# A transformer layer on one core: layernorm transposes two chunks later, quantisation steps moved, FFN weights loaded in the last round

## Chip, cores and metric

One Trainium2 (trn2) chip, one core. The metric is the device time of one execution in microseconds; the number given is the median of several runs. The profile is of one further execution of the same program.

## The reference

x is (4, 1024, 256) in float32, 16 heads of 128, FFN width 1024.

```python
xn = _layernorm(x)
q, k, v = split(einsum("bsd,od->bso", xn, w_qkv))       # 3 x 16 heads x 128
q, k = _apply_rope(q), _apply_rope(k)
attn = softmax(q @ k^T / sqrt(128))
a = (attn @ v).reshape(B, S, 2048) @ w_out^T
q_up, s_up = quantize_to_mxfp4(up_kernel)               # blocks of 32 along K
h = gelu(xn @ (q_up * s_up) + up_bias)
q_dn, s_dn = quantize_to_mxfp4(down_kernel)
out = x + a + h @ (q_dn * s_dn) + down_bias
```

## The kernel before

**Staging.** The attention part runs over 4 sequences x 8 pairs of heads. Two pairs make a round (ROUNDS = 16), and a round has 16 chunks, k = 0 to 15; a pair has 8 chunks, k8 = k % 8 (four chunks of 256 queries for each of its two heads). In `steps` the first four chunks stand alone, then a loop over rounds, then the last chunks; every engine runs its own `step(i, k, first, last)` in this order, tied to the others by semaphores alone. After the attention comes the FFN, 8 groups of 512 tokens.

**One chunk on TensorE** (line 1057 on): the first score tile of the next chunk (`next_scores(0)`), whatever stands in slot 0, the second score tile, `output(c - 2)`, whatever stands in slot 1, and `values(k - 1)`. Values of a chunk are therefore computed one chunk after its scores' exponentials, and its output projection another chunk later. Output waits for o_lo, the low part of the values, which VectorE makes.

**What stands in the slots.** The table GROUPS, written out by hand, says for (k8, slot) which projection group of the next pair runs there: twelve per pair (qk0 0 to 3, v 0 to 3, qk1 0 to 3), with the number that orders them. LN_SLOT (2, 1) holds the transposes of the layernorm of two token tiles for the next sequence, once a round. MX_SLOT (10, 1) holds the transposes of the FFN weights of this round, which VectorE has quantised in eight parts, one in each of the chunks 2 to 9 (MX_PARTS).

**VectorE in a chunk** (step, line 825 on), in this order: turn the probabilities of chunk k (L690, four stream transposes), low part of o of chunk c-2 (L702), the maxima of the two score tiles (L680), reciprocal (L697), add the output to y (L713). Between the two maxima of k = 2 stand newton (L735 to L741, four tiny instructions in a chain) and normalise (L747, two). Behind add_out stand the mean (k = 0) and the quantise part of the chunk. `variance` is at k = 1. Each part of quantise is one to five instructions, each waiting for the one ahead (`link`).

**ScalarE in a chunk**: high part of the weights (`w_high`: qk0 and v at k8 = 0, qk1 at 4), high part of o (L588), copies of the slots' results (`take_group`; for qk groups three instructions, L572 to L574, which hand over to GpSimd), the squares of the layernorm (k = 1), two exponentials (L582).

**GpSimd**: low parts of the weights (`w_low`, L475: qk0 and v at k8 = 0), the layernorm's guess (L487, k = 1), and for each qk group a rotation of five instructions (L460 to L467). Scores of a head wait until all of its groups are rotated (`qk_ready`).

**SyncE** issues all DMAs, in order. Per chunk eight key moves (L355); then the loads of weights of the pair after next, the layernorm's and quantiser's loads and stores at k = 5 and 12. The FFN's biases, x for the FFN (`load_x(0)`) and the two quantised weights come behind the last chunk (lines 414 to 423).

**Prologue**: ten projection groups of the first pair in FIRST_BANKS, ahead of the first scores. FIRST_HELD says which group must have been copied out before its bank is used again.

Of the kernel before, what the change touches and what calls it, by code (L numbers as in the profile page):

```python
# [8 lines left out]
F32 = mybir.dt.float32  # L9
# [7 lines left out]
BATCH, SEQ, DIM = 4, 1024, 256  # L17
HEADS, HEAD = 16, 128
FF = 1024
P = 128  # L20
# [9 lines left out]
PAIRS = BATCH * HEADS // 2  # L30
PAIRS_PER_SEQ = HEADS // 2
# [3 lines left out]
PAIR_GROUPS = 12  # L35
# [4 lines left out]
MX_COLS = 2 * DIM * FF // P  # L40
ROUNDS = PAIRS // 2
# [5 lines left out]
def layer(nc, d):  # L47
# [7 lines left out]
    with ExitStack() as ctx:  # L55
# [6 lines left out]
        def pb(name, shape):  # L62
# [36 lines left out]
        ln_x = sb("ln_x", [P, LN_STEP, DIM])  # L99
# [38 lines left out]
        o_ps = pb("o_ps", [P, 512])  # L138
        w_ps = pb("w_ps", [P, 512])
        FIRST_BANKS = [w_ps[:, :], o_ps[:, :], s_ps[1][:, 0:512], s_ps[1][:, 512:1024], slot_ps[:, 0], slot_ps[:, 1],  # L140
                       w_ps[:, :], o_ps[:, :], slot_ps[:, 0], s_ps[1][:, 0:512]]
        FIRST_HELD = {6: 0, 7: 1, 8: 4, 9: 2}

        const_loaded = sem("const_loaded")
        ident_loaded = sem("ident_loaded")
# [69 lines left out]

        GROUPS = {(3, 0): (0, "qk0", 0), (3, 1): (1, "qk0", 1), (4, 0): (2, "qk0", 2), (4, 1): (3, "v", 0),
                  (5, 0): (4, "qk0", 3), (5, 1): (5, "v", 1), (6, 0): (6, "v", 2), (6, 1): (7, "v", 3),
                  (7, 0): (8, "qk1", 0), (7, 1): (9, "qk1", 1), (0, 0): (10, "qk1", 2), (1, 0): (11, "qk1", 3)}  # L220
        FIRST_GROUPS = sorted(GROUPS.values())[:10]

        LN_SLOT, MX_SLOT = (2, 1), (10, 1)
        MX_PARTS = (2, 3, 4, 5, 6, 7, 8, 9)

        def group_at(k, slot, last):

# [55 lines left out]
        def _(sp):  # L283
            def load_part(p, pw, part, first=False):
                if not first:
                    sp.wait_ge(w_lo_ready[part], p)
                    sp.wait_ge(w_hi_ready[part], p)
                sp.dma_start(w_raw[:, :, PARTS[part]], d["w_qkv"][pw][:, :, PARTS[part]]).then_inc(w_loaded[part], 16)
# [25 lines left out]
            def load_mx(i):  # L314

                sp.dma_start(mx_raw[:, :], d["mx_rows"][:, bass.ds(i * MX_STEP, MX_STEP)]).then_inc(mx_loaded, 16)
# [42 lines left out]
            def batch(b, first, last):  # L359

                for n in range(SEQ_CHUNKS):
                    p, j, k8 = b * PAIRS_PER_SEQ + n // 8, n // 8, n % 8
                    r, k = b * SEQ_ROUNDS + n // 16, n % 16
                    move_chunk(b * SEQ_CHUNKS + n, n, first)
                    if not first:
                        if 1 <= n <= QUARTERS:
                            sp.wait_ge(y_stored, (b - 1) * (QUARTERS * 16) + 16 * n)
                            load_y(b, n - 1)
                        if n < QUARTERS:
                            store_y(b - 1, n)  # L370
                    if k8 == 1:
                        if j == PAIRS_PER_SEQ - 1 and not last:
                            sp.wait_ge(ln_stored, (b + 1) * (SEQ_ROUNDS * 32))
                            sp.wait_ge(proj_ready, (b + 1) * (PAIRS_PER_SEQ * PAIR_GROUPS))
                            load_x(b + 1)
                        if not (last and j >= PAIRS_PER_SEQ - 2):
                            load_part(p + 2, (j + 2) % PAIRS_PER_SEQ, "qk0")
                            load_part(p + 2, (j + 2) % PAIRS_PER_SEQ, "v")
                    if k8 == 5 and not (last and j >= PAIRS_PER_SEQ - 2):
                        load_part(p + 2, (j + 2) % PAIRS_PER_SEQ, "qk1")  # L380
                    if k8 == 4 and not (last and j == PAIRS_PER_SEQ - 1):
                        load_wo(p + 1, (j + 1) % PAIRS_PER_SEQ, 1)
                    if k8 == 7 and not (last and j >= PAIRS_PER_SEQ - 2):
                        load_wo(p + 2, (j + 2) % PAIRS_PER_SEQ, 0)
                    last_round = last and n // 16 == SEQ_ROUNDS - 1
                    if k == 5:
                        store_ln(r)
                        if not last_round:
                            load_ln(r + 1)
                    if k == 12:  # L390
                        store_mx(r)
                        if not last_round:
                            load_mx(r + 1)

            batch(0, True, False)
            for b in range(1, BATCH - 1):
# [14 lines left out]
                sp.wait_ge(rows_ready, (g + 1) * 2)  # L411
                sp.dma_start(d["out"][:, bass.ds(g * GT, GT), :], y_out[:, n]).then_inc(out_stored[n], 16)

            sp.dma_start(up_bias[:, :], d["up_bias"]).then_inc(bias_loaded, 16)
            sp.dma_start(down_bias[:, :], d["down_bias"].to_broadcast([P, DIM])).then_inc(bias_loaded, 16)
            sp.wait_ge(proj_ready, PAIRS * PAIR_GROUPS)
            sp.wait_ge(ln_stored, ROUNDS * 32)
            load_x(0)
            sp.wait_ge(mx_stored, ROUNDS * 16)
            for n in range(2):  # L420
                cols = slice(n * MX_COLS // 2, (n + 1) * MX_COLS // 2)
                dst = (up_w[:, :], down_w)[n]
                sp.dma_start(dst.bitcast(F32), d["mx"][:, cols]).then_inc(mx_w_loaded[n], 16)
            sp.wait_ge(scores_ready, TOK * HEADS // P)
            load_seq(1)
            load_seq(2)
# [43 lines left out]
        def _(pool):  # L470
# [31 lines left out]
            def step(i, k, first, last):  # L502
                if k >= 16:
                    return
                k8 = k % 8
                more = not (last and k >= 8)
                p = i * 2 + k // 8
                if k8 == 0 and more:
                    w_low(p + 1, "qk0")
                    w_low(p + 1, "v")  # L510
                if k8 == 3:
                    wo_low(p, 1)
                if k8 == 4 and more:
                    w_low(p + 1, "qk1")
                if k8 == 6 and more:
                    wo_low(p + 1, 0)
                if k == 1:
                    guess(i + 2, LN_COLS)
                for slot in (0, 1):
                    g = group_at(k, slot, last)  # L520
                    if g and g[1] != "v":
                        p = i * 2 + g[3]
                        rotate(pool, nc.gpsimd, p, g[1], g[2], "pool", p * 8 + qk_number(g[1], g[2]) - 3).then_inc(qk_ready, 1)
# [13 lines left out]
        def _(act):  # L537
            def w_high(p, part, first=False):

                cols = PARTS[part]  # L540
                act.wait_ge(w_loaded[part], (p + 1) * 16)
                if not first:
                    act.wait_ge(proj_ready, p * 12 - (0 if part == "qk1" else 4))
                nc.scalar.activation(w_hi[:, :, cols], w_raw[:, :, cols], ACT.Copy).then_inc(w_hi_ready[part], 1)

            def wo_high(p, h, first=False):
# [68 lines left out]
            def step(i, k, first, last):  # L615
# [4 lines left out]
                tail = last and k >= 16  # L620
                if k % 8 == 0 and more and not tail:
                    w_high(p + 1, "qk0")
                    w_high(p + 1, "v")
                if k % 8 == 3:
                    wo_high(p, 1, first)
# [15 lines left out]
                    act.wait_ge(mx_turned_ready, i + 1)  # L641
                    nc.scalar.activation(mx_turned[:, :], slot_ps[:, 1, 0:MX_STEP], ACT.Copy).then_inc(mx_copied, 1)
                if not tail:
                    if k == 1:
                        squares(i + 2, ln_x, LN_COLS)
                    if not (last and k == 15):
                        exponentials(t + 2, 2 * k + 2, first and k == 0)
                    g = group_at(k, 0, last)
                    if g:
                        take_group(i * 2 + g[3], *g[:3], g[3] % 2, slot_ps[:, 0])  # L650
                    if not (last and k == 15):
                        exponentials(t + 3, 2 * k + 3, first and k == 0)
                if k == 14:
                    act.wait_ge(ln_stored, (i + 1) * 32)
                    act.wait_ge(mx_stored, (i + 1) * 16)

# [19 lines left out]
        def _(dve):  # L676
# [152 lines left out]
            def step(i, k, first, last):  # L829
# [12 lines left out]
                                            ln_hi[:, :, :].bitcast(F32), ALU.subtract).then_inc(ln_lo_ready, 1)  # L842
                if not tail and not (last and k == 15):
                    row_max(t + 2, 2 * k + 2)
                if k == 1:
                    variance(LN_COLS, i * LN_STEP + BT)
                if k == 2:
                    newton(i + 2, LN_COLS)
                    normalise(i + 2, ln_x, ln_xn, LN_COLS)
                if not tail and not (last and k == 15):  # L850
                    row_max(t + 3, 2 * k + 3)
                if has_out:
                    invert(c - 2, 2 * k - 4)
                    add_out(c - 2, (k - 2) % 16, (i // 4) if k >= 2 else ((i - 1) // 4))
                if k == 0:
                    dve.wait_ge(ln_loaded, (i + 1) * 16)
                    mean(i + 2, ln_x, LN_COLS)
                if k in MX_PARTS:
                    quantise(i, MX_PARTS.index(k))

            steps(dve, step)

# [40 lines left out]
        def _(pe):  # L903
# [140 lines left out]
            pe.wait_ge(first_keys_pool, 1)  # L1044
            scores(0, 0, False)
            pe.wait_ge(rope_in, 6)
            pe.wait_ge(v_ready, 1)
            scores(1, 0, False)

            def step(i, k, first, last):  # L1050
# [11 lines left out]
                def slot(n):  # L1062
# [18 lines left out]
                        return  # L1081
                    place, part, num, ahead = g
                    if first and k == 0:
                        pe.wait_ge(rope_in, 6)
                        pe.wait_ge(v_ready, 4)
                    else:
                        bank_free(i, k, n, first, last)
                    if num == 0:
# [91 lines left out]
```

## Time and profile before

| | |
|---|---|
| median of 3 runs | 2652.19 us (2650.29 to 2653.58) |
| profiled execution, its own time | 2650.27 us |
| its span | 2648.5 us |
| PE busy | 2489.9 us, 94% |
| DVE busy | 2047.9 us, 77% |
| POOL busy | 1836.1 us, 69% |
| ACT busy | 1356.4 us, 51% |
| mean granted clock of TensorE | 0.979 |

The span goes from the first to the last instruction; the execution's own time has 1.8 us around it. PE is TensorE's matmuls, PEld its weight loads, DVE VectorE, ACT ScalarE, POOL GpSimd, SP SyncE and SPq its DMA queue. L702 is line 702 of the kernel. Many matmuls stand under the helper's line, L907, and are told apart by their tile: s_ps scores, w_ps output, o_ps values, slot_ps what runs in the slots. Busy times of PE are modelled at their ends and overlap a little with the next group's start, so PE's times are best read from start to start.

### The profile page before, as it was taken

The page shows a single profiled execution, that of the slowest core. Times are in us where ns is not written, and L with a number is a line of the kernel's source. Part 1 is how long each engine was busy: PE and PEld are TensorE (multiplying, and loading weights), DVE is VectorE, ACT ScalarE, POOL GpSimd, SP SyncE. Part 2 cuts the span into 40 slices and gives each one's busy share as a digit, 9 for nine tenths or more (in the row PEclk, how much of TensorE's full clock was granted, in tenths as well). Part 3 has the DMA queues.
Part 4 walks back from the last instruction along what each step waited for, and adds up shares of the span by engine and source line. Part 5 has one row for each costly group of instructions (what it writes and reads, how often), then busy time and mean ns, then how long its engine had stood idle before and what let it go on. Part 6 is the DMA issues. An engine that isn't in the chain of part 4 may idle for free. (4 is left out here: it accounts for less than half of the span.)

```text
span 2648.5 us, 42033 instructions
## 1 busy us (share of the span) xinstructions
PE 2489.9 (94%) x12656; PEld 2157.4 (81%) x12656; DVE 2047.9 (77%) x3209; ACT 1356.4 (51%) x2518; POOL 1836.1 (69%) x1480
## 2 busy tenths in 40 slices
PE   5999999999999999999999999999999999999799
PEld 4887878888787888878788887878888787887688
DVE  6868778786877878787787878778687877868676
ACT  5555545555554555555455555545555454554333
POOL 6677767867776776787677678767767876776221
PEclk9999999999999999999999999999999999999999
DMA  3555545545654554546555454546555454544642
GB/s 105 135 132 132 136 105 153 129 119 162 161 138 105 150 128 121 132 127 169 136 152 128 121 134 125 138 110 171 137 150 136 123 138 112 144 121 111 189 172 64
DMA packets 233732, 354.30 MB, mean 134 GB/s; under 512 B 37840, under 2 KB 95440, under 8 KB 233424
## 3 DMA queue, kind: packets, MB, share of 16 engines
q1 hardware_dynamic: 233680, 353.72, 51.5%
q8 instruction: 18, 0.29, 0.0%
q14 instruction: 34, 0.28, 0.0%
HBM read 66.26 MB, written 18.87 MB: 32 GB/s over the span
## 5 line engine op out<-in xcount | busy, mean ns | idle before, releaser
L907 PE MATMUL o_ps<-keys_first,v_rows 128*128 128x256 f32 x4096 | 950.9, 386 | 0.0
L582 ACT ACTIVATE probs<-s_ps,neg_max 128x1024 f32<-128x1024 f32 x512 | 571.2, 1116 | 664.2 <-DVE neg_max L680 658.2
L680 DVE TENSOR_REDUCE neg_max<-s_ps 128x1 f32<-128x1024 f32 x512 | 621.5, 1219 | 341.9 <-PE s_ps L907 341.5
L907 PEld LDWEIGHTS o_ps<-keys_first,v_rows 128*128 128x128 f32 x4096 | 782.9, 195 | 105.9
L907 PE MATMUL s_ps<-seq_parts 128*128 128x512 f32 x3072 | 828.6, 407 | 36.9 <-POOL seq_parts L467 25.4
L907 PEld LDWEIGHTS s_ps<-seq_parts 128*128 128x128 f32 x3072 | 575.0, 188 | 160.7 <-POOL seq_parts L467 31.4
L460 POOL TENSOR_TENSOR rope_a<-rope_a,cos 128x512 f32<-128x512 f32 x253 | 329.4, 1302 | 541.6 <-ACT rope_b L574 541.6
L690 DVE STREAM_TRANSPOSE turned_blocks<-probs 128x512 f32<-128x512 f32 x1024 | 637.3, 679 | 26.5 <-DVE mx_inv L778 9.9
L907 PE MATMUL slot_ps<-seq_parts,w_parts 128*128 128x512 f32 x1512 | 388.7, 392 | 1.5 <-ACT probs L574 1.5
L588 ACT ACTIVATE o_hi<-o_ps 128x256 fp32r<-128x256 f32 x256 | 98.5, 385 | 525.2 <-PE o_ps L907 525.2
L465 POOL TENSOR_TENSOR rope_a<-rope_a,rope_b 128x512 f32<-128x512 f32 x253 | 330.7, 1307 | 19.8
L463 POOL TENSOR_TENSOR seq_parts<-rope_a,rope_b 128x512 fp32r<-128x512 f32 x253 | 327.8, 1296 | 19.8
L467 POOL TENSOR_TENSOR seq_parts<-rope_a,seq_parts 128x512 fp32r<-128x512 f32 x253 | 327.0, 1292 | 19.8
L461 POOL TENSOR_TENSOR rope_b<-rope_b,sin 128x512 f32<-128x512 f32 x253 | 330.6, 1307 | 0.0
L907 PEld LDWEIGHTS slot_ps<-seq_parts,w_parts 128*128 128x128 f32 x1512 | 280.6, 189 | 59.9 <-issue 1.7
L713 DVE SCALAR_TENSOR_TENSOR y<-w_ps,inv_sum,y 128x256 f32<-128x256 f32 x512 | 224.4, 480 | 45.3 <-PE w_ps L907 17.0
L702 DVE TENSOR_TENSOR o_lo<-o_ps,o_hi 128x256 fp32r<-128x256 f32 x256 | 102.9, 402 | 130.8 <-ACT o_hi L588 130.8
L907 PE MATMUL slot_ps<-w_parts,seq_parts 128*128 128x256 f32 x1500 | 200.3, 283 | 0.0
L907 PEld LDWEIGHTS slot_ps<-w_parts,seq_parts 128*128 128x128 f32 x1500 | 191.0, 191 | 2.6
L573 ACT ACTIVATE rope_b<-slot_ps 64x512 f32<-64x512 f32 x251 | 149.3, 595 | 3.0
L574 ACT ACTIVATE rope_b<-slot_ps 64x512 f32<-64x512 f32 x251 | 148.1, 590 | 2.9
L572 ACT ACTIVATE rope_a<-slot_ps 128x512 f32<-128x512 f32 x251 | 148.0, 590 | 1.2 <-DVE seq_parts L467 1.2
(109 smaller groups left out, 2159.2 us busy)
## 6 DMA issues: line engine op xcount, KB each, us to landing
keys_first<-turned_blocks SPq DMA_DIRECT2D x2048, 128.0 KB, 2.7
w_raw<-in_w_qkv SPq DMA_DIRECT2D x96, 256.0 KB, 3.2
seq_parts<-xnt_parts SPq DMA_DIRECT2D x14, 1024.0 KB, 7.9
wo_raw<-in_w_out SPq DMA_DIRECT2D x64, 128.0 KB, 2.5
y<-in_x SPq DMA_DIRECT2D x16, 256.0 KB, 3.2
ln_x<-in_x SPq DMA_DIRECT2D x16, 256.0 KB, 3.8
xnt_parts<-ln_hi SPq DMA_DIRECT2D x16, 256.0 KB, 3.3
xnt_parts<-ln_lo SPq DMA_DIRECT2D x16, 256.0 KB, 3.6
```

The source lines that it names most:

```text
L460: engine.tensor_tensor(a, a, cos[:, cols], ALU.mult).then_inc(own, 1)
L461: engine.tensor_tensor(b, b, sin[:, cols], ALU.mult).then_inc(own, 1)
L463: engine.tensor_tensor(hi, a, b, ALU.add).then_inc(own, 1)
L465: engine.tensor_tensor(a, a, b, ALU.add).then_inc(own, 1)
L467: return engine.tensor_tensor(lo, a, hi.bitcast(F32), ALU.subtract)
L573: nc.scalar.activation(b[0:h], bank[h:P], ACT.Copy, scale=scale)
L574: nc.scalar.activation(b[h:P], bank[0:h], ACT.Copy, scale=scale).then_inc(rope_in, 1)
L582: nc.scalar.activation(probs[:, k2 % 4, :], s_ps[k2 % 2][:, :], ACT.Exp, bias=neg_max[:, col:col + 1], accum_out=row_sum[:, col:col + 1]). ...
L680: nc.vector.tensor_reduce(neg_max[:, k2 % 16:k2 % 16 + 1], s_ps[k2 % 2][:, :], AXX, ALU.max, negate=True).then_inc(max_ready, 1)
L690: last = nc.vector.transpose(turned_blocks[:, k % 2, 2 * half:2 * half + 2, :, n, :].rearrange("p b j q -> p j b q"), keys)
L713: last = nc.vector.scalar_tensor_tensor(rows, w_ps[:, n * DIM:(n + 1) * DIM], inv_sum[:, col:col + 1], rows, ALU.mult, ALU.add)
L907: ins = nc.tensor.matmul(out, w, m, start=(n == 0), stop=(n == len(terms) - 1))
```

## The change

- GROUPS: v 0 goes from (4, 1) to (5, 1), v 1 from (5, 1) to (6, 0), v 2 from (6, 0) to (6, 1), and v 3 from (6, 1) into the next pair, to (0, 1). The prologue has nine groups.
- LN_SLOT goes from chunk 2 to chunk 4. The mean goes from k = 0 to 1, the squares, variance and guess from 1 to 2. Newton and normalise go from k = 2, between the maxima, to k = 3, behind add_out. The store and next load of the layernorm go from k = 5 to 6.
- MX_PARTS: the eight parts stand in the chunks 3 to 7: 0 and 1 at 3, then 2, 3, 4 and 5, 6 and 7.
- The v part of the weights is loaded at k8 = 3 (was 1) and split at k8 = 2 (was 0).
- The loads of the FFN's biases, of x and of the FFN weights are issued at k = 10, 11 and 13 of the last round, and not behind it. ScalarE's wait for the stores goes from k = 14 to 15.

```diff
-        GROUPS = {(3, 0): (0, "qk0", 0), (3, 1): (1, "qk0", 1), (4, 0): (2, "qk0", 2), (4, 1): (3, "v", 0),
-                  (5, 0): (4, "qk0", 3), (5, 1): (5, "v", 1), (6, 0): (6, "v", 2), (6, 1): (7, "v", 3),
-                  (7, 0): (8, "qk1", 0), (7, 1): (9, "qk1", 1), (0, 0): (10, "qk1", 2), (1, 0): (11, "qk1", 3)}
-        FIRST_GROUPS = sorted(GROUPS.values())[:10]
-
-        LN_SLOT, MX_SLOT = (2, 1), (10, 1)
-        MX_PARTS = (2, 3, 4, 5, 6, 7, 8, 9)
+        GROUPS = {(3, 0): (0, "qk0", 0), (3, 1): (1, "qk0", 1), (4, 0): (2, "qk0", 2), (5, 0): (3, "qk0", 3),
+                  (5, 1): (4, "v", 0), (6, 0): (5, "v", 1), (6, 1): (6, "v", 2), (7, 0): (7, "qk1", 0),
+                  (7, 1): (8, "qk1", 1), (0, 0): (9, "qk1", 2), (0, 1): (10, "v", 3), (1, 0): (11, "qk1", 3)}
+        FIRST_GROUPS = sorted(GROUPS.values())[:9]
+
+        USED = {"qk0": 4, "v": 11, "qk1": 12}
+
+        LN_SLOT, MX_SLOT = (4, 1), (10, 1)
+        MX_PARTS = {3: (0, 1), 4: (2,), 5: (3,), 6: (4, 5), 7: (6, 7)}
...
                             load_part(p + 2, (j + 2) % PAIRS_PER_SEQ, "qk0")
-                            load_part(p + 2, (j + 2) % PAIRS_PER_SEQ, "v")
+                    if k8 == 3 and not (last and j >= PAIRS_PER_SEQ - 2):
+                        load_part(p + 2, (j + 2) % PAIRS_PER_SEQ, "v")
...
-                    if k == 5:
+                    if k == 6:
                         store_ln(r)
...
+                    if last_round and k == 10:
+                        sp.dma_start(up_bias[:, :], d["up_bias"]).then_inc(bias_loaded, 16)
+                        sp.dma_start(down_bias[:, :], d["down_bias"].to_broadcast([P, DIM])).then_inc(bias_loaded, 16)
+                    if last_round and k == 11:
+                        sp.wait_ge(proj_ready, PAIRS * PAIR_GROUPS)
+                        sp.wait_ge(ln_stored, ROUNDS * 32)
+                        load_x(0)
+                    if last_round and k == 13:
+                        sp.wait_ge(mx_stored, ROUNDS * 16)
+                        for m in range(2):
+                            cols = slice(m * MX_COLS // 2, (m + 1) * MX_COLS // 2)
+                            dst = (up_w[:, :], down_w)[m]
+                            sp.dma_start(dst.bitcast(F32), d["mx"][:, cols]).then_inc(mx_w_loaded[m], 16)
...
                 if k8 == 0 and more:
                     w_low(p + 1, "qk0")
+                if k8 == 2 and more:
                     w_low(p + 1, "v")
...
-                if k == 1:
+                if k == 2:
                     guess(i + 2, LN_COLS)
...
-                if k == 1:
+                if k == 2:
                     variance(LN_COLS, i * LN_STEP + BT)
-                if k == 2:
-                    newton(i + 2, LN_COLS)
-                    normalise(i + 2, ln_x, ln_xn, LN_COLS)
                 if not tail and not (last and k == 15):
                     row_max(t + 3, 2 * k + 3)
                 if has_out:
                     invert(c - 2, 2 * k - 4)
                     add_out(c - 2, (k - 2) % 16, (i // 4) if k >= 2 else ((i - 1) // 4))
-                if k == 0:
+                if k == 1:
                     dve.wait_ge(ln_loaded, (i + 1) * 16)
                     mean(i + 2, ln_x, LN_COLS)
-                if k in MX_PARTS:
-                    quantise(i, MX_PARTS.index(k))
+                if k == 3:
+                    newton(i + 2, LN_COLS)
+                    normalise(i + 2, ln_x, ln_xn, LN_COLS)
+                for part in MX_PARTS.get(k, ()):
+                    quantise(i, part)
```

ScalarE's `w_high` of v goes to k8 = 2 and its squares to k = 2, as the same kind of edit; in the prologue TensorE's waits for the copies of v follow the new order.

## Rows read from the trace of the kernel before

**Rows 1.** The page, part 1: busy us, share of the span, instructions.
```profile
PE 2489.9 (94%) x12656; PEld 2157.4 (81%) x12656; DVE 2047.9 (77%) x3209; ACT 1356.4 (51%) x2518; POOL 1836.1 (69%) x1480
```

**Rows 2.** Waits: engine, line, waited for: us in total, times, longest.
```profile
PE slot_ps L1068 <- DVE ln_xn L747: 86.5, 16, 5.6
...
PE s_ps L907 <- POOL seq_parts L467: 25.4, 15, 1.7
...
PE s_ps L1008 <- DMA up_w<-mx_blocks: 12.6, 1, 12.6
```

**Rows 3.** Timeline of PE: transposes, scores of chunk 3, transposes a round later.
```profile
687.32 1.12 PE L1068 MATMUL slot_ps<-ident,ln_xn 128*128 128x128 f32 x4 [5.59 <-DVE ln_xn L747]
...
692.43 1.75 PE L907 MATMUL s_ps<-seq_parts 128*128 128x512 f32 x6
...
841.45 1.12 PE L1068 MATMUL slot_ps<-ident,ln_xn 128*128 128x128 f32 x4 [5.60 <-DVE ln_xn L747]
```

**Rows 4.** Windows: length, busy time by engine, granted clock, DMA share, GB/s.
```profile
687.30:692.43 5.13, 5.11 (x20) 4.47 (x21) 4.70 (x10) 1.51 (x3) 0.72 (x1) 0.73 0.26 93
```

**Rows 5.** Timeline of PE, chunk 4: scores, output, v group, values.
```profile
702.11 1.72 PE L907 MATMUL s_ps<-seq_parts 128*128 128x512 f32 x6
...
706.39 0.28 PE L907 MATMUL w_ps<-wo_hi,o_hi 128*128 128x256 f32 x1
...
707.11 1.60 PE L907 MATMUL slot_ps<-w_parts,seq_parts 128*128 128x256 f32 x12
708.55 3.62 PE L907 MATMUL o_ps<-keys_first,v_rows 128*128 128x256 f32 x16
```

**Rows 6.** Timeline of PE: output of chunk 10, scores of chunk 11.
```profile
760.59 0.39 PE L907 MATMUL w_ps<-wo_hi,o_hi 128*128 128x256 f32 x1
...
766.94 1.66 PE L907 MATMUL s_ps<-seq_parts 128*128 128x512 f32 x6 [1.70 <-POOL seq_parts L467]
```

**Rows 7.** Timeline of POOL: low parts of qk0 and v at k8 = 0.
```profile
751.04 2.54 POOL L475 TENSOR_TENSOR w_parts<-w_raw,w_parts 128x512 fp32r<-128x512 f32 x2
```

**Rows 8.** Timeline of DVE: newton to the next maxima, part 0, part 1, two turns.
```profile
680.82 1.07 DVE L735 TENSOR_TENSOR ln_step<-ln_guess 128x2 f32<-128x2 f32 x1
681.92 1.19 DVE L737 TENSOR_TENSOR ln_step<-ln_step,ln_var 128x2 f32<-128x2 f32 x1
...
687.18 1.21 DVE L680 TENSOR_REDUCE neg_max<-s_ps 128x1 f32<-128x1024 f32 x1
...
689.51 0.28 DVE L768 TENSOR_SCALAR mx_abs<-mx_raw 128x256 uint32<-128x256 uint32 x1
...
690.39 2.49 DVE L690 STREAM_TRANSPOSE turned_blocks<-probs 128x512 f32<-128x512 f32 x4
...
699.13 0.74 DVE L772 TENSOR_SCALAR mx_amax<-mx_amax 128x8 f32<-128x8 f32 x1
...
703.11 2.49 DVE L690 STREAM_TRANSPOSE turned_blocks<-probs 128x512 f32<-128x512 f32 x4 [0.66 <-DVE mx_inv L778]
...
757.75 2.48 DVE L690 STREAM_TRANSPOSE turned_blocks<-probs 128x512 f32<-128x512 f32 x4
```

**Rows 9.** Single lines: least/median/most ns, first and last start, forms.
```profile
L737 DVE TENSOR_TENSOR ln_step<-ln_step,ln_var x18: 161/1186/1191, 9.6 to 2384.2; 128x2 f32<-128x2 f32 x16, 128x4 f32<-128x4 f32 x2
...
L764 DVE SCALAR_TENSOR_TENSOR mx_q<-mx_abs,mx_q x96: 411/907/1520, 100.0 to 2450.9; 128x256 f32<-128x256 f32 x96
```

**Rows 10.** Timeline of POOL: beside newton, and the first rotation of chunk 3.
```profile
681.83 1.27 POOL L461 TENSOR_TENSOR rope_b<-rope_b,sin 128x512 f32<-128x512 f32 x1
...
698.56 1.28 POOL L460 TENSOR_TENSOR rope_a<-rope_a,cos 128x512 f32<-128x512 f32 x1 [7.82 <-ACT rope_b L574]
```

**Rows 11.** Key moves of the last three chunks (SyncE), and all key moves' landing.
```profile
2482.57 18.94 SPq L355 DMA_DIRECT2D keys_first<-turned_blocks  x24
...
DMA to landing us min/median/max: 2.5/2.7/7.1
```

**Rows 12.** Timeline of PE, first round, scores at k = 1.
```profile
54.10 2.93 PE L907 MATMUL s_ps<-seq_parts 128*128 128x512 f32 x6 [9.65 <-ACT probs L582]
```

More of the change, by code:

```diff
@@ L140, in layer @@
         FIRST_BANKS = [w_ps[:, :], o_ps[:, :], s_ps[1][:, 0:512], s_ps[1][:, 512:1024], slot_ps[:, 0], slot_ps[:, 1],
-                       w_ps[:, :], o_ps[:, :], slot_ps[:, 0], s_ps[1][:, 0:512]]
-        FIRST_HELD = {6: 0, 7: 1, 8: 4, 9: 2}
+                       w_ps[:, :], o_ps[:, :], s_ps[1][:, 0:512]]
+        FIRST_HELD = {6: 0, 7: 1, 8: 2}
         const_loaded = sem("const_loaded")
@@ L412, in store_rows @@
                 sp.dma_start(d["out"][:, bass.ds(g * GT, GT), :], y_out[:, n]).then_inc(out_stored[n], 16)
[L414 to L423, printed above, removed]
             sp.wait_ge(scores_ready, TOK * HEADS // P)
@@ L542, in w_high @@
                 if not first:
-                    act.wait_ge(proj_ready, p * 12 - (0 if part == "qk1" else 4))
+                    act.wait_ge(proj_ready, (p - 1) * 12 + USED[part])
                 nc.scalar.activation(w_hi[:, :, cols], w_raw[:, :, cols], ACT.Copy).then_inc(w_hi_ready[part], 1)
@@ L622, in step @@
                     w_high(p + 1, "qk0")
+                if k % 8 == 2 and more:
                     w_high(p + 1, "v")
@@ L652, in step @@
                         exponentials(t + 3, 2 * k + 3, first and k == 0)
-                if k == 14:
+                if k == 15:
                     act.wait_ge(ln_stored, (i + 1) * 32)
@@ L844, in step @@
                     row_max(t + 2, 2 * k + 2)
-                if k == 1:
+                if k == 2:
                     variance(LN_COLS, i * LN_STEP + BT)
-                if k == 2:
-                    newton(i + 2, LN_COLS)
-                    normalise(i + 2, ln_x, ln_xn, LN_COLS)
                 if not tail and not (last and k == 15):
@@ L1046, in _ @@
             pe.wait_ge(rope_in, 6)
-            pe.wait_ge(v_ready, 1)
             scores(1, 0, False)
@@ L1083, in slot @@
                     if first and k == 0:
-                        pe.wait_ge(rope_in, 6)
-                        pe.wait_ge(v_ready, 4)
+                        pe.wait_ge(v_ready, n + 1)
                     else:
```

## The prediction, made before the changed kernel was run

> **What bounds the kernel now.** The first view to read is the busy time by engine: PE 2489.9 us of a span of 2648.5 [rows 1]. So the time is PE's work and PE's waits, and another engine counts only where it makes PE wait. The second view is the waits [rows 2]: three cost PE something. Once a round, sixteen times, the layernorm transposes wait for VectorE's ln_xn, 86.5 us together; 5.59 each [rows 3], so that 2.7 is left for the first round. Fifteen times scores wait 1.7 us for the rotation on GpSimd, 25.4 together. Once the FFN waits 12.6 us for the load of up_w. VectorE (77%) is no bound on average, but it works in order, and a burst of work on it makes it late.
>
> The third view is PE's timeline in a steady round. Call Sk the start of the first scores of chunk k. The transposes of k=2 start at 687.32, those of the next round at 841.45: a round is 154.1 us [rows 3]. The fourth view is the windows: behind the wait the granted clock is 0.73 for 5.13 us, that is partly 1.2 GHz instead of 2.4 after PE had stood idle; 5.13 x 0.27 = 1.4 us lost besides [rows 4].
>
> **Part by part.** PE does the same twelve groups per pair and the same transposes; work 0. What moves is one v group, 708.55 - 707.11 = 1.44 us [rows 5], from chunks 4 and 12 to 0 and 8.
>
> *The wait for GpSimd.* At k=11 scores waited 1.70 us for the last instruction of the last qk1 rotation [rows 6]. The change takes the low part of v, half of 2.54 = 1.27 us [rows 7], from ahead of that rotation, and PE comes 1.44 later by the v group that now stands at k=8. 1.70 - 1.27 - 1.44 = -1.0: the wait goes, and it does not appear at k=3, where the other wait hid it until now and where the guess too has left its place. Gain 25 us. With rotations slowed by VectorE some of it could stay: bounds 18 and 25.
>
> *The wait for ln_xn* at k=2 goes: 86.5 us, and the low clock behind it, 15 x 1.4 = 21.
>
> *What is late next.* VectorE's step 3 now ends with newton, normalise and quantise parts 0 and 1, one behind the other. Their prices, each up to the start of what came behind: newton and normalise 687.18 - 680.82 = 6.36; part 0 690.39 - 689.51 = 0.88; part 1 703.11 - 699.13 = 3.98, 0.66 of it idle for its last link [rows 8]. Sum 11.2. They are so dear because GpSimd works beside them: L737 takes 161 ns at least but 1186 in the median [rows 9], and it ended at 683.11 as GpSimd's instruction of 681.83 did, at 683.10 [rows 8, 10]. GpSimd works in step 3 as well: it starts the rotation of (3, 0) at S3 + 6.13 (698.56 - 692.43), and that of (3, 1) follows, ten instructions of 1.3 us [rows 3, 10]. VectorE's added work starts at S3 + 6.70 (699.13 - 692.43). So I take the dear prices. Part 0 stood beside an idle GpSimd until now; if its first instruction has to wait too, the sum is 11.8. I take 11.4.
>
> Who waits for that: VectorE begins step 4 at S3 + 18.1. Ahead of the low part of o it turns the probabilities; from the start of the turn at 757.75 to PE's output matmul at 760.59 it was 2.84 [rows 6, 8]. So output starts at S3 + 20.9, which is S4 + 11.3, as chunk 3 lasts 9.68 (702.11 - 692.43). PE gets there at S4 + 4.28 (706.39 - 702.11) [rows 3, 5]. It stalls 7.0 us in each round, and will show this as "w_ps waits for o_lo". 16 x 7.0 = 112 us, and the low clock behind it, 16 x 1.4 = 22. Queued behind the output on PE are the transposes (which find ln_xn long ready), the values and the next scores; ScalarE and VectorE wait for these in turn, so that the whole chunk ends 7 us later and VectorE has caught up. With what went, a round is again about 154 us.
>
> The Trainium skill, "SBUF — State Buffer", section "Who interferes with whom", has a rule that speaks against this change: GpSimd and some VectorE instructions (two SBUF inputs, or a tensor_scalar in a fast form) share a port pair under an exclusive lock, the loser is blocked for a whole instruction, and tensor_reduce never is. By that rule nine added instructions of step 3 wait for one of GpSimd's each: an estimate of 9 x 1.3 and 0.9 for the others, 12.6, and a stall of 8.2.
>
> *Later chunks.* Step 4 keeps part 2; VectorE begins step 5 about when PE begins chunk 5, and its turn is covered until S5 + 4.28. Steps 5, 6 and 7 have two, four and four instructions of quantise. L764, the commonest, takes 0.91 us in the median [rows 9]: 3.6 for four. From 6.7 into the chunk, and with 2.84 for the turn, output could start 13.2 after Sk, where PE comes at 9.7 + 4.28 = 14.0. No second stall, by 0.8 us.
>
> *Queues of ScalarE and SyncE.* ScalarE, 51% busy [rows 1], has w_high of v and the squares one or two chunks later; both fall in time in which it waits for the maxima: 0. Its wait for the stores comes at k=15, three chunks behind them: 0. SyncE issues the v load behind the key moves of chunk 3; 24 key moves took 18.9 us, at most 6.3 a chunk [rows 11], of chunks that last 9.7 where the v load stands, and the load is used a pair later: 0. Uncovered it would be some 3 us, once a pair.
>
> *Start.* A v projection leaves the prologue. PE then waits 9.65 us all the same for ScalarE's exponentials behind VectorE's rotation [rows 12], so 0; bounds -3 and +2, since ScalarE's copies change their order.
>
> *End.* x and the FFN weights are loaded at k=11 and 13, not behind the key moves of chunk 15. The 12.6 us of [rows 2] go, and about 1.3 of low clock. But 4 MB now run beside the key moves of chunks 12 to 14, and values wait for those; a key move landed in 2.7 us in the median, 7.1 at most [rows 11]. Bounds of the loss: 0, and twice 4.4. I take 2. Gain 12.
>
> **Sum**, against the profiled execution's own 2650.3 us (the span and 1.8 around it; the median of the runs is 1.9 above it): -86.5 - 21 - 25 + 112 + 22 - 12 = -10.5, so 2639.8, and 2641.7 on the median's scale. As starts measured from start to start lose slightly more than the idle times I took off, I round this down to 2640. One microsecond of the stall is worth 16.
>
> **Rivals.**
> (a) *The added work hides.* If GpSimd did not hold VectorE up, the small instructions would cost 0.2 us and the wide ones 0.41 [rows 9], about 3.5 in all: output could start at S3 + 6.7 + 3.5 + 0.7 + 2.8 = S4 + 4.0, ahead of PE. The 134 us are not added: 2506. For it: the chunks from 3 on are the long ones. Against it: the same instructions beside the same rotation in [rows 8, 10]. Cases half-way, some instructions slipping in between two of GpSimd's, give 2560 to 2600. Chance 0.14 together.
> (b) *Slower: a second stall.* Its place is steps 6 and 7 with four quantise instructions each. At the 1.52 that L764 takes at most [rows 9] each step has 6.1 instead of 3.6: output is ready 15.6 after Sk, 1.6 late, once or twice a round, less what the first lateness covers. From 0.9 us a round on, first stall or second, all the gain and 0.2% more is gone. With 1.5: 2640 + 24 = 2664. Against it: in chunk 6 GpSimd has ended its rotations before VectorE comes to the quantise parts. Chance 0.13.
> (c) *No change.* The loads of the end hold the key moves up by twice 4.4 us, and 0.3 us of the rotation wait stays: 2640 + 7 + 5 = 2652. Chance 0.12.
> My forecast has 0.61. That the transposes were not moved off the wait can be left out: by the sum ln_xn is ready 8 us before them.
>
> **Numbers.** A measurement of this kernel can tell 0.2%, 5 us, from no change. The stall's bounds are 5.8 (small instructions slipping in) and 8.2: -19 and +19 us; clock 0.8 to 2.0 a stall, -10 and +10; the end -2 and +7. Together 2615 to 2664. The range goes down for part of the half-way cases and holds (c) and half of (b): 2598 to 2664. Faster: 0.44 of my forecast's 0.61, (a) 0.14, a little of (c), in all 0.62. Same 0.22, slower 0.16.
>
> **What would show it.** Right: PE waits neither for ln_xn nor for GpSimd's seq_parts; sixteen waits of w_ps for o_lo of about 7 us, all at k=4; L735 starts 6.7 us after S3, L737 still takes 1.2, the turn of step 4 starts 18 after S3; up_w is there before PE. Wrong: a round of 145 to 147 us (a: I priced step 3 wrongly); waits for o_lo more than once a round (b); values waiting for key moves in the last chunks (c); or another waiter than output at k=4, the second scores for instance, which would mean that I named the wrong path.

## The result, and the profile after

The changed kernel takes 2656.39 us (median of 20 runs, 2649.71 to 2660.54), the kernel before 2651.16 (20 runs, 2649.97 to 2653.58). The ratio is 1.0016, with a 95% interval of 1.0010 to 1.0023: slower, by 0.16%. The forecast was 2640, so nearly half a percent faster. The profiled execution took 2657.86 us, with a span of 2656.1.

The page's busy times of the changed kernel, to set against [rows 1]:

```profile
PE 2497.0 (94%) x12656; PEld 2166.2 (82%) x12656; DVE 2038.3 (77%) x3209; ACT 1357.1 (51%) x2518; POOL 1826.7 (69%) x1480
```

PE does the same 12656 matmuls, with the same share of the span. What changed is the list of its waits (engine, line, waited for: us in total, times, longest), to set against [rows 2]:

```profile
PE w_ps L915 <- DVE o_lo L710: 123.6, 33, 7.4
PE s_ps L1042 <- DVE probs L755: 14.3, 2, 12.2
PE s_ps L915 <- ACT probs L589: 7.1, 1, 7.1
PE o_ps L915 <- DMA keys_first<-turned_blocks: 4.1, 2, 3.3
PE s_ps L915 <- DVE seq_parts L473: 3.2, 1, 3.2
```

All three waits of [rows 2] that cost PE something are gone: 86.5 + 25.4 + 12.6 = 124.5 us. In their place PE waits 123.6 us for o_lo, which was 1.0 before: 16 waits of 6.9 to 7.4 at the output of chunk 4 and 16 of some 0.34 at chunk 8, one of each a round. The timeline of PE in a steady round shows where: chunk 4 (S4 = 702.73) and chunk 8.

```profile
702.73 1.72 PE L915 MATMUL s_ps<-seq_parts 128*128 128x512 f32 x6
...
714.54 0.58 PE L915 MATMUL w_ps<-wo_hi,o_hi 128*128 128x256 f32 x1 [7.37 <-DVE o_lo L710]
...
721.84 1.74 PE L915 MATMUL s_ps<-seq_parts 128*128 128x512 f32 x6
...
755.87 0.39 PE L915 MATMUL w_ps<-wo_hi,o_hi 128*128 128x256 f32 x1 [0.34 <-DVE o_lo L710]
```

Scores in chunks 3 (693.06) and 4 start without a wait, so GpSimd's last rotation is in time. The output of chunk 4 waits 7.37 us. VectorE's timeline of the same stretch says why. Read each start against the one ahead of it: from newton's first instruction at 699.75, right behind add_out, to the turn at 711.61 stands one chain of thirteen instructions, and only behind the turn comes o_lo (L710).

```profile
699.75 0.61 DVE L743 TENSOR_TENSOR ln_step<-ln_guess 128x2 f32<-128x2 f32 x1
700.39 1.20 DVE L745 TENSOR_TENSOR ln_step<-ln_step,ln_var 128x2 f32<-128x2 f32 x1
701.62 0.17 DVE L747 TENSOR_SCALAR ln_step<-ln_step 128x2 f32<-128x2 f32 x1
...
702.97 2.83 DVE L755 TENSOR_SCALAR ln_xn<-ln_x,ln_mean,ln_rstd 128x256 f32<-128x256 f32 x2
705.73 1.38 DVE L776 TENSOR_SCALAR mx_abs<-mx_raw 128x256 uint32<-128x256 uint32 x1
...
711.61 2.49 DVE L698 STREAM_TRANSPOSE turned_blocks<-probs 128x512 f32<-128x512 f32 x4 [0.66 <-DVE mx_inv L786]
714.03 0.39 DVE L710 TENSOR_TENSOR o_lo<-o_ps,o_hi 128x256 fp32r<-128x256 f32 x1
```

Step 3's chain starts 6.69 us after S3 and lasts 11.86. GpSimd's timeline beside it: the rotation of (3, 0) runs from 699.07 on, instruction by instruction, and L745 ends at 701.59 as GpSimd's instruction of 700.30 does at 701.57. Not every instruction is held up: L747 starts at 701.62, between the end of one of GpSimd's at 701.57 and the start of the next at 701.65, and takes 0.17 us.

```profile
699.07 1.28 POOL L466 TENSOR_TENSOR rope_a<-rope_a,cos 128x512 f32<-128x512 f32 x1 [4.37 <-ACT rope_b L581]
700.30 1.27 POOL L467 TENSOR_TENSOR rope_b<-rope_b,sin 128x512 f32<-128x512 f32 x1
701.65 1.26 POOL L469 TENSOR_TENSOR seq_parts<-rope_a,rope_b 128x512 fp32r<-128x512 f32 x1
```

At chunk 8 the small wait has the same form: parts 6 and 7 stand beside the rotation of (7, 0), whose first instruction starts at 747.41, and the turn comes late.

```profile
748.23 0.61 DVE L803 TENSOR_SCALAR mx_raw<-mx_raw 128x256 uint32<-128x256 uint32 x1
748.76 1.49 DVE L772 SCALAR_TENSOR_TENSOR mx_q<-mx_abs,mx_q 128x256 f32<-128x256 f32 x1
...
753.02 2.48 DVE L698 STREAM_TRANSPOSE turned_blocks<-probs 128x512 f32<-128x512 f32 x4
```

**The account by stages**, each between two landmarks of PE that both kernels have (before minus after, spans of 2648.5 and 2656.1):

| stage | before | after | difference |
|---|---|---|---|
| start, to the scores of k=2 of the first round | 63.71 | 65.95 | +2.2 |
| rounds, to the mx transposes of the last | 2400.63 | 2414.95 | +14.3 |
| from there to the first down matmul | 61.56 | 52.58 | -9.0 |
| FFN, to the end | 122.6 | 122.6 | 0 |

### The profile page after: what moved, and what is told of

It is laid out like the page before. It is cut to its first block and busy times, and to the rows that moved or that the text cites. A ratio compares the mean times of both kernels' runs of the same rounds, so it can differ in the third digit from the quotient of the medians.

```text
span 2656.1 us, 41956 instructions
## 1 busy us (share of the span) xinstructions
PE 2497.0 (94%) x12656; PEld 2166.2 (82%) x12656; DVE 2038.3 (77%) x3209; ACT 1357.1 (51%) x2518; POOL 1826.7 (69%) x1480
## 5 line engine op out<-in xcount | busy, mean ns | idle before, releaser
L915 PE MATMUL w_ps<-wo_hi,o_hi 128*128 128x256 f32 x512 | 152.4, 298 | 123.7 <-DVE o_lo L710 123.6
L915 PEld LDWEIGHTS w_ps<-wo_hi,o_hi 128*128 128x128 f32 x512 | 100.9, 197 | 147.0 <-issue 116.5
L710 DVE TENSOR_TENSOR o_lo<-o_ps,o_hi 128x256 fp32r<-128x256 f32 x256 | 104.2, 407 | 128.2 <-ACT o_hi L595 125.7
L580 ACT ACTIVATE rope_b<-slot_ps 64x512 f32<-64x512 f32 x250 | 148.7, 595 | 3.0
```

The costliest lines, as they stand in the source:

```text
L580: nc.scalar.activation(b[0:h], bank[h:P], ACT.Copy, scale=scale)
L710: nc.vector.tensor_tensor(as_queries(o_lo[:, slot, :]), as_quadrants(o_ps[:, 0:CHUNK]), as_queries(o_hi[:, slot, :].bitcast(F32)), ALU.sub ...
L915: ins = nc.tensor.matmul(out, w, m, start=(n == 0), stop=(n == len(terms) - 1))
```

## The experiments

Every run stands beside runs of the kernel before on the same chip, whose medians were 2650.8 to 2651.9 us.

**Is GpSimd what makes the chain long?** The rotations of slots (3, 0) and (3, 1) work on 8 columns instead of 512, so that most of these query and key parts are left out; VectorE's program is the same.

```diff
-    rotate(pool, nc.gpsimd, p, g[1], g[2], "pool", p * 8 + qk_number(g[1], g[2]) - 3).then_inc(qk_ready, 1)
+    rotate(pool, nc.gpsimd, p, g[1], g[2], "pool", p * 8 + qk_number(g[1], g[2]) - 3,
+           8 if k == 3 else HALF).then_inc(qk_ready, 1)
```

> The changed kernel, but the GpSimd rotations of the groups in slots (3, 0) and (3, 1) of each round work on 8 columns instead of 512 (most of these query and key parts are left out). VectorE's work in step 3 is untouched. Theory (GpSimd holds VectorE up): the chain behind add_out shrinks from 11.9 to about 4 us, output of chunk 4 no longer waits, 2495 to 2520 us. Rival (VectorE's chain is that long by itself): the chain stays 11 to 12 us, the stall stays at 7, about 2650 us.

Measured: 2500.1 us, ratio 0.9434 (0.9418 to 0.9449). VectorE's timeline of step 3:

```profile
658.09 0.15 DVE L744 TENSOR_TENSOR ln_step<-ln_guess 128x2 f32<-128x2 f32 x1
...
658.88 0.73 DVE L756 TENSOR_SCALAR ln_xn<-ln_x,ln_mean,ln_rstd 128x256 f32<-128x256 f32 x2
659.53 0.29 DVE L777 TENSOR_SCALAR mx_abs<-mx_raw 128x256 uint32<-128x256 uint32 x1
...
661.15 0.17 DVE L787 TENSOR_SCALAR mx_inv<-mx_inv 128x8 f32<-128x8 f32 x1
661.99 2.49 DVE L699 STREAM_TRANSPOSE turned_blocks<-probs 128x512 f32<-128x512 f32 x4 [0.67 <-DVE mx_inv L787]
```

The same instructions take 3.90 us instead of 11.86, GpSimd's beside them 0.2 us each, and the wait of chunk 4 is gone. This settles the question: two thirds of the chain was time in which GpSimd held VectorE up. The Trainium skill's rule of the exclusive port pair ("SBUF — State Buffer", "Who interferes with whom") agrees with this pair of runs, also in that the reduction among them kept its 0.42 us. By the rule the prediction had estimated 12.6 us for the chain, 0.7 above the 11.86 of the trace, in which L747 and L782 passed at 0.17 us each.

**Which work belongs where?** Newton and normalise put between the two maxima of chunk 3, where GpSimd is idle:

```diff
                 if k == 2:
                     variance(LN_COLS, i * LN_STEP + BT)
+                if k == 3:
+                    newton(i + 2, LN_COLS)
+                    normalise(i + 2, ln_x, ln_xn, LN_COLS)
                 if not tail and not (last and k == 15):
                     row_max(t + 3, 2 * k + 3)
...
-                if k == 3:
-                    newton(i + 2, LN_COLS)
-                    normalise(i + 2, ln_x, ln_xn, LN_COLS)
```

> The changed kernel with newton and normalise of step 3 put between the two maxima of chunk 3, where GpSimd is idle (its low parts end 1.6 us after S3, its rotation starts 6.0 after it) and VectorE waits 1.5 us for scores anyway. Theory (VectorE's chain in step 3 is dear because GpSimd's rotation holds it up): L745 falls from 1.2 us to about 0.2 and L755 from 1.4 to 0.4; only parts 0 and 1 (5.9 us) are left behind add_out, the stall of w_ps at k=4 shrinks from 7.4 to about 2 us and most of the low clock behind it goes: about 2540 us. Rival (the chain is dear by itself, whatever GpSimd does): L745 and L755 stay, the second maximum comes 4.5 us late, the stall stays at about 6: about 2640 us.

Measured: 2517.7 us, ratio 0.9498 (0.9482 to 0.9514), 22 better than expected. VectorE's timeline in chunk 3:

```profile
658.27 0.15 DVE L743 TENSOR_TENSOR ln_step<-ln_guess 128x2 f32<-128x2 f32 x1
658.45 0.16 DVE L745 TENSOR_TENSOR ln_step<-ln_step,ln_var 128x2 f32<-128x2 f32 x1
...
659.05 0.74 DVE L755 TENSOR_SCALAR ln_xn<-ln_x,ln_mean,ln_rstd 128x256 f32<-128x256 f32 x2
659.87 1.23 DVE L688 TENSOR_REDUCE neg_max<-s_ps 128x1 f32<-128x1024 f32 x1
```

Newton and normalise take 1.6 us, in place of 5.98, and fill a gap in which VectorE had waited for scores. The stall at k=4 is 0.8 us, 1.2 less than the 2 expected, which is 19 us in sixteen rounds. Half of that is parts 0 and 1, which I took at their full 5.9 and which came to 5.3.

**The other half: quantise moved away from chunk 3**, newton left behind add_out:

```diff
-        MX_PARTS = {3: (0, 1), 4: (2,), 5: (3,), 6: (4, 5), 7: (6, 7)}
+        MX_PARTS = {4: (0,), 5: (1,), 6: (2, 3, 4), 7: (5,), 8: (6,), 9: (7,)}
```

> The changed kernel with the quantise parts spread over chunks 4 to 9 (part 0 at 4, 1 at 5, 2 to 4 at 6, 5 at 7, 6 at 8, 7 at 9), none in chunk 3. Theory (the lateness is the length of the chain in step 3): newton and normalise alone take 6.0 us, the stall at k=4 becomes 6.7 + 6.0 + 2.9 - 13.95 = 1.6 us, the 0.34 at k=8 goes: about 2530 us. Rival (the layernorm sets the stall and the quantiser only fills idle time): stall unchanged near 7, about 2650 us.

Measured: 2528.2 us, ratio 0.9534 (0.9518 to 0.9550). Its stall at k=4 is 1.47 us (expected 1.6), and it has 0.3 us at k=10:

```profile
676.21 0.38 PE L915 MATMUL w_ps<-wo_hi,o_hi 128*128 128x256 f32 x1 [1.47 <-DVE o_lo L710]
676.42 0.28 PE L915 MATMUL w_ps<-wo_lo,o_hi 128*128 128x256 f32 x1
...
677.46 3.62 PE L915 MATMUL o_ps<-keys_first,v_rows 128*128 128x256 f32 x16
680.72 1.75 PE L915 MATMUL s_ps<-seq_parts 128*128 128x512 f32 x6
```

Behind this short wait the next matmuls soon stand 0.12 us apart and the values take 3.26 us, full clock, and so in all sixteen rounds. Either half alone removes most of the loss, as neither half of the chain is long enough by itself to pass the cover of 4.4 us by much. That is why the halves' gains (139 and 128 us) do not add up.

**Both edits together.**

> Both edits: newton and normalise between the maxima of chunk 3, quantise spread over chunks 4 to 9. Theory: no step of VectorE is late, no wait of PE in the steady rounds, a round of about 145 us instead of 155.3: 2656 - 16 x 10.2 = about 2493 us. Rival (another limit stands close behind, for example GpSimd's rotation ahead of the scores of k=3 or the key moves): a round of 148 us or more, 2540 us or more, with a wait of another name.

Measured: 2501.5 us, ratio 0.9432 (0.9416 to 0.9448). No wait at k=4, a round of 145.4 us. The expectation of 2493 left out 0.32 us at k=10 in every round, the place that e2 had shown too, and the start, whose scores of k=2 come at 64.66 us in this profile and at 62.81 in e4_narrow's.

**Parts 6 and 7 both in chunk 8**, which is a long chunk since it holds a v group:

```diff
-        MX_PARTS = {4: (0,), 5: (1,), 6: (2, 3, 4), 7: (5,), 8: (6,), 9: (7,)}
+        MX_PARTS = {4: (0,), 5: (1,), 6: (2, 3, 4), 7: (5,), 8: (6, 7)}
```

> As e3_both, but quantise parts 6 and 7 both in chunk 8, which is a long one now, and none in 9. Theory: the last wait of a steady round, 0.32 us at the output of chunk 10 behind part 7 of chunk 9, goes with nothing in its place: 145.0 us a round, 16 x 0.4 = 7 us less than e3_both, about 2495 us. Rival (parts 6 and 7 together are too long for step 8): a wait at the output of chunk 9 instead, 2501 us or more.

Measured: 2493.7 us, ratio 0.9407 (0.9393 to 0.9422). The busy time of PE over fifteen rounds (window; length, busy time by engine, clock, DMA share, GB/s):

```profile
83.90:2259.50 2175.60, 2173.59 (x11133) 1892.64 (x11132) 1701.05 (x2836) 1217.69 (x2281) 1702.25 (x1366) 1.00 0.56 143
```

PE idles 2 us in 2176, nearly all of it in three waits for a load of seq_parts, 1.9 us together. That is what is left to gain by waits in the rounds: next to nothing. A round has 145.0 us, and so the 154.1 of [rows 3] held 9 to 10 us of stalls and low clock, of which the change had merely renamed the most part.

**Does an idle PE pay twice?** In the changed kernel 24 matmuls that nobody reads run ahead of chunk 4's output, in PE's idle time:

```diff
+                if k == 4:
+                    bank_free(i, k, 1, first, last)
+                    for m in range(24):
+                        nc.tensor.matmul(slot_ps[:, 1], qk_hi[:, 1, 0, 0:P], qk_hi[:, 1, 1, 0:HALF], start=True, stop=True)
                 if not (first and k < 2):
                     output(c - 2, (k - 2) % 16, i * 2 + (k - 2) // 8, first and k == 2)
```

> The changed kernel with 24 more matmuls of 512 columns (a scores product once more, written to the free slot bank and never read) ahead of the output of chunk 4, in time in which PE stands idle for o_lo. Nothing else is changed. Theory (the idle time costs a second time, through the granted clock behind it, about 2.3 us a round): output, transposes and values of chunk 4 take 4.4 us instead of 6.2 to 7.3, a round is 153 us, about 2620 us, although PE does 82 us more work. Rival (low clock is not due to the idle time, or the added work delays the output): 2656 us or more.

Measured: 2626.4 us, ratio 0.9908 (0.9893 to 0.9923). PE does more and is 30 us faster than in the changed kernel. Its longest wait for o_lo is 2.1 us now, and the mean granted clock of the core is 0.995 where it was 0.970.

```profile
PE w_ps L915 <- DVE o_lo L710: 37.9, 33, 2.1
```

The low clock behind the wait is thus worth about 30 us a run, 1.9 a round. It is not gone everywhere: in four of the sixteen rounds output, transposes and values still take 6.1 us behind a wait of 2.0, in the others 4.5. For the changed kernel the windows behind the wait of chunk 4 show it, here in a steady round and in the first:

```profile
714.54:721.84 7.30, 7.30 (x26) 6.40 (x27) 6.20 (x11) 4.08 (x7) 3.21 (x3) 0.60 0.72 189
94.10:101.01 6.91, 6.91 (x26) 6.14 (x27) 6.19 (x11) 4.08 (x7) 2.82 (x3) 0.64 0.70 171
```

Long and short stretches take turns: the one a round after the first of these, from the output at 870.38 to the next scores at 876.58, takes 6.20 us at a granted clock of 0.71. At full clock the same output, transposes and values take 4.4 us, so that the low clock costs 1.5 to 2.9 us a round.

**The loads of the end by themselves**, on the kernel before:

```diff
+                    if last_round and k == 11:
...
+                        load_x(0)
+                    if last_round and k == 13:
...
-            load_x(0)
-            sp.wait_ge(mx_stored, ROUNDS * 16)
```

> The kernel before with only the loads of the end moved into the last round (biases at k=10, x at 11, FFN weights at 13). Theory: from the mx transposes of the last round to the first down matmul the changed kernel took 52.6 us instead of 61.6, so this part alone is worth 9 us: about 2642 us, the wait for up_w gone, 3 to 4 us of values waiting for key moves in its place. Rival (the gain came with the rest of the change): 2651 us, or no waits for key moves at all and 2639.

Measured: 2642.3 us, ratio 0.9968 (0.9955 to 0.9981). The change's end part alone is worth 8.5 us, and values wait 3.0 us for key moves, here at the two chunks whose moves run beside the loads. The eight moves issued behind the two loads of x landed in 7.4 us in the median, where 2.7 was the median of all in the kernel before:

```profile
2489.97 5.41 PE L911 MATMUL o_ps<-keys_first,v_rows 128*128 128x256 f32 x16 [2.41 <-DMA keys_first<-turned_blocks]
...
2504.87 3.72 PE L911 MATMUL o_ps<-keys_first,v_rows 128*128 128x256 f32 x16 [0.58 <-DMA keys_first<-turned_blocks]
```

**The start.** Twelve idle matmuls ahead of the first scores of the changed kernel, while PE waits for the rotation:

```diff
+            for m in range(12):
+                nc.tensor.matmul(s_ps[0][:, 0:HALF], x_hi[:, 0, 0:P], x_hi[:, 0, 0:HALF], start=True, stop=True)
             pe.wait_ge(first_qk_dve, 2)
```

> The changed kernel with 12 idle matmuls of 512 columns ahead of the first scores, into their own bank, in time in which PE waits 3.2 us for the rotation. Theory (the start lost 2.2 us since PE, with one group less, stood idle and had the low clock from 34 us on): the twelve matmuls of the second scores take 3.0 us instead of 5.3, the scores of k=2 start about 2 us earlier, 2654 us. Rival (the new order of ScalarE's copies made the start late): the start stays, 2656 us.

Measured: 2654.4 us (11 runs), ratio 1.0015 (1.0006 to 1.0024). The interval covers the changed kernel's, so the median does not tell the two apart. The traces do differ. The changed kernel, and then this one:

```profile
38.87 5.49 PE L915 MATMUL s_ps<-seq_parts 128*128 128x512 f32 x12 [0.80 <-ACT rope_b L581]
...
65.95 3.10 PE L915 MATMUL s_ps<-seq_parts 128*128 128x512 f32 x12
```

```profile
38.19 3.00 PE L915 MATMUL s_ps<-seq_parts 128*128 128x512 f32 x12 [2.07 <-ACT rope_b L581]
...
62.66 3.08 PE L915 MATMUL s_ps<-seq_parts 128*128 128x512 f32 x12
```

The scores of the second tile ran at low clock in the changed kernel's profiled execution and at full clock here, and k=2 starts 3.3 us earlier. But the other traces spread as widely without this edit. With the changed prologue as it is, k=2 starts at 62.3 to 62.8 us in five of them (e1_between, e4_narrow, e6_busy_wait, e8_spread, e8_again) and at 65.05 and 64.66 in e2_quant_away and e3_both; with the prologue of before it starts at 63.71 and, in e5_end_loads_only, at 65.41. Low clock in the twelve matmuls is not enough for a late start: in e8_spread they took 4.25 us, and k=2 came at 62.30. In the three late traces of the changed prologue the first six score matmuls, from 35 us on, had also run at low clock, 2.8 to 2.9 us instead of 1.67. So the start differs from one execution to the next by as much as the 2.2 us of the account; that the change costs anything there is not shown.

**Both ends mended**: e8_spread with the start of e7 and with down_w loaded at k=14.

> e8_spread with both ends mended: the twelve idle matmuls of e7_start_busy ahead of the first scores, and the second FFN weight (down_w) loaded at k=14 of the last round instead of behind up_w at k=13. Theory: e8's profile already had the full clock at its start, so the first edit is worth 0 to 3 us in the median; the second takes 1 to 2 us from the 4.4 us in which values wait for key moves, since each load then stands beside the moves of one chunk: 2489 to 2493 us. Rival (the key moves wait for the bytes ahead of them, whatever their order, or down_w comes late for the first down matmul): 2494 us or more, with the same 4.4 us or a new wait of s_ps for w_parts.

Measured: 2491.9 us, ratio 0.9401 (0.9386 to 0.9417). Beside it:

> e8_spread once more, beside e9_ends on the same chip: 2493 us in the median, to be set against e9_ends.

Measured: 2495.4 us, ratio 0.9409 (0.9393 to 0.9425). The waits of values for key moves, first e9_ends, then e8_again:

```profile
PE o_ps L915 <- DMA keys_first<-turned_blocks: 2.7, 4, 1.2
```

```profile
PE o_ps L915 <- DMA keys_first<-turned_blocks: 7.4, 2, 5.0
```

The wait is shorter and the medians differ by 3.5 us, but the intervals overlap, and e8_spread, the same kernel as e8_again, waited 4.4 us for key moves and had a median of 2493.7. So a gain by the later load is possible, not shown. The idle matmuls brought nothing that the traces show: k=2 starts at 63.38 in e9_ends and at 62.81 in e8_again. The expectation also took e8_spread's start for one at full clock, which its twelve matmuls of 4.25 us were only in part. e9_ends has the lowest median found, 6% below both kernels, and it leaves out nothing of the computation.

## Why the prediction was wrong

*The mechanism was right, point by point.* The waits for ln_xn, for GpSimd's rotation and for up_w went. VectorE's step 3 became late, its added work started at S3 + 6.69 (forecast 6.70), and PE stalled at the output of chunk 4, once a round, for o_lo. Rival (a), that the added work hides, was refused by the trace, and e4_narrow shows its condition: with GpSimd's instructions cut to 0.2 us beside the chain it does hide, at 2500 us (2506 was worked out). Of rival (c) the hold-up of key moves came, at 4.1 of its 8.8 us; its rest of the rotation wait did not.

*The sum came out 18 us low*, 2639.8 against 2657.9 on the profiled execution's scale (14.7 us on the scale of the medians). The time lies in the stated range, but on the other side of the kernel before than forecast. The terms that were mis-sized, by the account above:

- **The stall at k=4**: 7.53 us from start to start (714.54 - 702.73 - 4.28), not 7.0. The chain took 11.86, where I took 11.4, between the 11.2 of the old places and the 11.8 for the case that part 0's first instruction has to wait. L776 (part 0) indeed went from 0.28 to 1.38. The turn to output took 2.93, not 2.84. Together 8.5 us in sixteen rounds. The upper of my own two values was right in kind, because it alone counted part 0 beside a busy GpSimd; that it was right to 0.1 us was luck, as part 0 came 1.0 dearer (1.87 for 0.88) and newton and normalise 0.4 cheaper (5.98 for 6.36).
- **"No second stall, by 0.8 us"** failed at k=8: 0.34 us of wait, 0.5 from start to start, 8 us in all. That is rival (b) at a third of its price. I had priced the four instructions of parts 6 and 7 at L764's median, 3.6 us; beside the rotation of (7, 0) they took 4.8, from 748.23 to the turn at 753.02. A median over places beside busy and idle GpSimd is no price for a place beside a busy one.
- **The low clock** I took from one round, 1.4 us a time (5.13 x 0.27). The next round before shows 6.53 us from transposes to scores (841.45 to 847.98) for work of 3.7, so 2.8, and the one behind that 5.58 (996.98 to 1002.56), so 1.9: I had taken the cheapest of three kinds that come in turn; from the mean rounds, 154.8 and 155.3 us against e8_spread's 145, less the stalls, it is 2.0 before and 2.3 after. As it came and went again, the error nearly cancelled: about +5 us.
- **The waits removed** were taken at their idle time instead of from start to start: 2.04 for 1.70 and 5.75 for 5.59, some 7 us to the good. I had seen this and rounded for it, but by 2 us only.
- **The end** gave 9.0, not 12, as values waited 0.78 and 3.28 us for key moves, and took 5.05 us behind the second wait, at a granted clock of 0.66, where they take 3.26 at full clock: 3 us.

```profile
2502.82 3.72 PE L915 MATMUL o_ps<-keys_first,v_rows 128*128 128x256 f32 x16 [0.78 <-DMA keys_first<-turned_blocks]
...
2518.68 5.41 PE L915 MATMUL o_ps<-keys_first,v_rows 128*128 128x256 f32 x16 [3.28 <-DMA keys_first<-turned_blocks]
```

- **The start** lost 2.2 in this pair of traces, just beyond its bound of +2. As e7_start_busy shows, single traces of one prologue differ by as much.

For the rounds this makes 8.5 + 8 + 5 - 7 = 14.5 us; the account shows 12.8 (14.3 against my +1.5). The ends add 3 + 2.2. The sign was decided by terms of 0.5 us a round. With a gain of 10.5 us left between sums of 144.5 and 134 us, a chance of 0.62 for faster was too high: the error of one priced chain, sixteenfold, was 8.5 us, nearly as large as the gain. That the low clock and the waits removed, mis-sized as well, moved the sum by only 5 and 7 us, and in opposite directions, was luck.

## What to carry to other kernels

Price a VectorE instruction by what GpSimd does at its new place, one by one, and not by its median; in a burst of tiny dependent VectorE instructions beside a working GpSimd most cost one GpSimd instruction each (here thirteen took the time of nine). Before moving work to "a long chunk", look at which third of the chunk GpSimd is idle: here the same six instructions cost 1.6 us between the maxima and 6.0 behind add_out. When one wait of an in-order engine is removed, work out when the next result that it needs is due, with the removed wait gone: here the wait for ln_xn at k=2 became one for o_lo at k=4.

## What the runs showed of the hardware

A chain of thirteen VectorE instructions took 3.9 us beside GpSimd instructions of 0.2 us (e4_narrow) and 11.9 beside ones of 1.3 us back to back (the changed kernel); an instruction on 8 elements a partition (L784, in e4_narrow L785) took 0.17 and 1.1 us, while two that started between the end of one of GpSimd's and the start of the next (L747, L782) took 0.17 beside the busy GpSimd too. Waits of 7.4 us of TensorE were followed by 6.0 to 7.4 us at granted clocks of 0.60 to 0.74; behind waits of 1.5 us (e2_quant_away) the following matmuls ran at full clock in all sixteen rounds, behind waits of 2.0 us (e6_busy_wait) not in four of them. Filling the idle time with matmuls that nobody reads brought 30 us. Key moves of 128 KB landed in 7.4 us in the median behind two loads of 1 MB (e5_end_loads_only), against 2.7.
